# An RK4 loop with an FFN in its slots: the unclipped q goes through PSUM, the seed goes ahead of the clip, and five FFN sums move from GpSimd to VectorE

## The reference, cut to what matters

```
def _derivative(q, p, drive, coupling, bias):
    dq = q - q ** 3 / 3.0 - p + drive + jnp.tanh(q) @ coupling.T + bias
    dp = EPSILON * (q + ALPHA - BETA * p)
...
q_next = q + DT / 6.0 * (dq1 + 2 * dq2 + 2 * dq3 + dq4)
q_next = jnp.clip(q_next, -CLAMP, CLAMP)          # CLAMP = 20, the same for p_next
...
qx, sx, sc = _reorder_quantize_x(xf, up_reorder_index)      # fp8 rounding, one scale a row
g = _qlinear(qx, sx, sc, w_gate, ...); u = _qlinear(qx, sx, sc, w_up, ...)
t = jax.nn.silu(g) * u
qt, st, sct = _reorder_quantize_x(t, down_reorder_index)
y = _qlinear(qt, st, sct, w_down, down_reorder_index)
```

## Time and profile before

| | |
|---|---|
| median of 3 runs | 1775.01 us (1772.31 to 1779.2) |
| the profiled execution, its own time | 1778.82 us, span 1777.0 us |
| TensorE busy | 1558.6 us, 88% |
| VectorE busy | 1146.7 us, 65% |
| ScalarE busy | 486.2 us, 27% |
| GpSimd busy | 383.7 us, 22% |
| DMA | 70.26 MB, mean 40 GB/s |

### The profile page before, as it was taken

How to read it: one execution, slowest core, us unless ns; L and a number is a source line. 1 busy time by engine, 2 the same in 40 slices (tenths; PEclk the granted TensorE clock), 3 DMA queues, 4 the chain that set the end, 5 groups by cost and what they waited for, 6 DMA issues and landing times.

```text
span 1777.0 us, 44630 instructions
## 1 busy us (share of the span) xinstructions
PE 1558.6 (88%) x16703; PEld 960.7 (54%) x16744; DVE 1146.7 (65%) x3063; ACT 486.2 (27%) x1333; POOL 383.7 (22%) x554
## 2 busy tenths in 40 slices
PE   5999899998869999999999996778788888888884
PEld 2333333333747667676676744555565555555552
DVE  2888633335687556475664713478888888888885
ACT  1323211112020210202102012344444444444442
POOL 1221000000000000000000001245455445545554
PEclk9999999999879999999999998899999999999997
DMA  7232200005000000000000032011111111111111
GB/s 302 72 83 72 62 24 12 12 10 107 1 0 1 24 6 18 24 0 24 6 18 24 0 118 94 20 29 32 34 34 30 32 30 32 30 30 36 38 29 36
DMA packets 88431, 70.26 MB, mean 40 GB/s; under 512 B 30728, under 2 KB 80824, under 8 KB 87352
## 3 DMA queue, kind: packets, MB, share of 16 engines
q1 hardware_dynamic: 86616, 63.75, 12.5%
q0 software_dynamic: 1760, 5.77, 1.2%
HBM read 52.55 MB, written 16.92 MB: 39 GB/s over the span
## 4 chain that ended last, share of the span: by engine, by line
PE 66%; DVE 17%; issue 7%; ACT 5%; DMA 2%; SPq 1%; POOL 1%; DVEq 1%; ACTq 0%; POOLq 0%
PE ps L681 12%; PE ps L671 12%; PE ps L774 12%; PE ps L588 9%; PE ps L596 8%; DVE mem L1311 4%; PE ps L715 3%; PE ps L739 2%; DVE mem L1318 2%; ACT ps L955 2%; DVE ps L1289 2%; ACT mem L962 2%; DMA mem<-in_xT 1%; DVE mem L1322 1%; PE ps L692 1%
## 5 line engine op out<-in xcount | busy, mean ns | idle before, releaser
L774 PE MATMUL ps<-mem 128*32 128x128 f32 x8192 | 284.5, 280 | 122.2 <-ACT mem L962 55.1
L774 PEld LDWEIGHTS ps<-mem 128*32 128x32 f32 x8192 | 220.2, 111 | 196.1 <-issue 119.5
L671 PE MATMUL ps<-mem 128*128 128x512 f32 x512 | 224.6, 592 | 0.0
L681 PE MATMUL ps<-mem 128*128 128x256 f32 x1024 | 222.3, 379 | 0.0
L681 PEld LDWEIGHTS ps<-mem 128*128 128x128 f32 x1024 | 193.9, 190 | 26.0
L514 POOL TENSOR_TENSOR mem<-mem 128x128 f32<-128x128 f32 x64 | 31.2, 487 | 802.5 <-ACT mem L958 802.5
L588 PE MATMUL ps<-mem 128*32 128x384 f32 x2048 | 184.2, 502 | 0.0
L596 PE MATMUL ps<-mem 128*32 128x384 f32 x2048 | 177.1, 486 | 2.7 <-DVE mem L1120 2.7
L671 PEld LDWEIGHTS ps<-mem 128*128 128x128 f32 x512 | 95.6, 190 | 109.7 <-issue 109.3
L518 POOL TENSOR_TENSOR mem<-mem 128x128 f32<-128x128 f32 x192 | 103.7, 540 | 191.5 <-ACT mem L958 185.4
L765 PE MATMUL ps<-mem 128*128 128x128 f32 x768 | 141.0, 308 | 0.0
(11 more groups left out here) (128 smaller groups left out, 2103.5 us busy)
## 6 DMA issues: line engine op xcount, KB each, us to landing
mem<-x_scr SPq DMA_DIRECT2D x128, 64.0 KB, 1.9
mem<-in_xT SPq DMA_DIRECT2D x64, 64.0 KB
mem<-in_Wq SPq DMA_DIRECT2D x1, 4096.0 KB
mem<-in_Wo SPq DMA_DIRECT2D x1, 4096.0 KB
mem<-in_x SPq DMA_DIRECT2D x16, 256.0 KB, 2.7
x_scr<-mem SPq DMA_DIRECT2D x32, 128.0 KB, 2.3
q_scr<-mem SPq DMA_DIRECT2D x64, 64.0 KB, 1.6
mem<-q_scr SPq DMA_DIRECT2D x64, 64.0 KB, 1.9
```

The source lines that it names most:

```text
L671: mm = pe.matmul(ps[:, 6 + pr, :], aoT[:, h, pr * P:pr * P + P], wo[:, h, :], start=(h == 0), stop=(h == HEADS - 1))
L681: mm = pe.matmul(ps[:, h % Q_BANKS, 0:BLK], wq[:, c, h * DH:(h + 1) * DH], xnb[:, c, :], start=(c == 0), stop=(c == NC - 1))
L774: mm = pe.matmul(ps[32 * j:32 * j + 32, st % 2, 0:P], thT[:, c, :], ct[:, c, j * P:(j + 1) * P], start=False, stop=(c == NC - 1), skip_gro ...
```

## The change

In the fourth stage the new q is written to an unused part of PSUM bank 4 instead of the SBUF tile `qpre`. The transpose and the clip read it there. The seed of the next step's first stage is issued ahead of the clip, no longer at the start of the next stage. Five sums of a tile leave POOL for VectorE: the two of 512 columns of the q rounding (now slots 8 and 9), the two `t_rounded` halves of 768 and 640 columns (slots 13 and, one group on, 0) and the last sum with x1 (slot 14 instead of 11). POOL keeps the sums of p and `gate_scaled`.

```diff
--- before.py
+++ after.py
@@ -247,7 +247,7 @@
         qst = [f32(w.take(P), P) for _ in range(3)]
         qsT = f32(w.take(P), NC, B)
         thT = f32(w.take(P), NC, B)
-        ebuf, qpre, pacc = (f32(w.take(P), P) for _ in range(3))
+        ebuf, pacc = (f32(w.take(P), P) for _ in range(2))
         pw = [f32(w.take(P), P) for _ in range(5)]
         qt = f32(w.take(D), D)
         x1t = f32(w.take(D), D)
@@ -528,39 +528,15 @@
                 pool.wait_ge(f_sig, GU_T * i + m + 1)
                 pool.tensor_tensor(sig[m % 2], sig[m % 2], us_row[:, m * GU_N:(m + 1) * GU_N], ALU.mult).then_inc(f_sgu, 1)
 
-            def t_rounded(i, half):
-
-                lo, hi = T_PARTS[half]
-                pool.wait_ge(f_ta, 2 * i + half + 1)
-                wait_if(pool, f_tT, 2 * i + half - 1)
-                pool.tensor_tensor(t8[:, lo:hi], vt[:, lo:hi], et[:, lo:hi], ALU.subtract).then_inc(f_t8, 1)
-
             def slot(k, tile):
                 i = tile(0)
                 if i is not None:
-                    if k == 7:
-                        pool.wait_ge(f_xe, i + 1)
-                        pool.tensor_tensor(vq, vq, eq, ALU.add).then_inc(f_xa, 1)
-                    if k == 8:
-                        pool.wait_ge(f_xa, i + 1)
-
-                        wait_if(pool, f_qT, i)
-                        pool.tensor_tensor(qx8, vq, eq, ALU.subtract).then_inc(f_q8, 1)
                     if k in (13, 14):
                         gate_scaled(i, k - 13)
                 i = tile(1)
                 if i is not None:
                     if k in (1, 3):
                         gate_scaled(i, 2 + k // 2)
-                    if k in (12, 15):
-                        t_rounded(i, k // 15)
-                i = tile(2)
-                if i is not None and k == 11:
-                    pool.wait_ge(f_ysc, i + 1)
-                    pool.wait_ge(x1_ld, 16 * TILE_T * (i + 1))
-
-                    wait_if(pool, o_wr, PRIMED + 16 * TILE_T * i)
-                    pool.tensor_tensor(yout, ysc, x1t, ALU.add).then_inc(f_out, 1)
 
             def group(g, rk, tile):
                 for k in range(16):
@@ -1289,6 +1265,7 @@
                     dve.scalar_tensor_tensor(out=o, in0=p, scalar=float(SEEDS[st][0]), in1=driven(s), op0=ALU.mult, op1=ALU.add).then_inc(rk_seed, 1)
 
             drive_sum(0, 0, 1)
+            seed(0, 0, 0)
 
             def stage(g, s, st, last, fill):
                 t = 4 * g + s
@@ -1296,8 +1273,6 @@
                 qs = qn[(s - 1) % 4] if st == 0 else qst[st - 1]
                 stt = dve.scalar_tensor_tensor
                 end = last and s == 3
-                if st == 0:
-                    seed(t, s, 0)
                 dve.wait_ge(rk_sq, n + 1)
                 stt(out=ebuf, in0=ps[:, 5, 0:P], scalar=KEPT[st], in1=qs, op0=ALU.subtract, op1=ALU.mult).then_inc(rk_e, 1)
                 if st < 3:
@@ -1307,7 +1282,7 @@
                     drive_sum(t + 1, (s + 1) % 4, g + 1 + (s == 3))
                 dve.wait_ge(rk_e, n + 1)
                 dve.wait_ge(rk_mm, n + 1)
-                dst = qst[st] if st < 3 else qpre
+                dst = qst[st] if st < 3 else ps[:, 4, 2 * P:3 * P]
                 stt(out=dst, in0=ps[:, st % 2, 0:P], scalar=STEP[st], in1=ebuf, op0=ALU.mult,
                     op1=ALU.subtract).then_inc(rk_qs if st < 3 else rk_pre, 1)
                 if st < 3:
@@ -1317,9 +1292,11 @@
                 if not (end and st == 3):
                     dve.transpose(qsT.rearrange("p c b -> p (c b)"), dst).then_inc(rk_qT, 1)
                 if st == 3:
+                    if not end:
+                        seed(t + 1, (s + 1) % 4, 0)
 
                     wait_if(dve, q_wr[s], PRIMED + 16 * g)
-                    dve.tensor_scalar(qn[s], qpre, CLAMP, -CLAMP, ALU.min, ALU.max).then_inc(rk_qs, 1)
+                    dve.tensor_scalar(qn[s], dst, CLAMP, -CLAMP, ALU.min, ALU.max).then_inc(rk_qs, 1)
 
             def slot(v, k, tile):
 
@@ -1341,6 +1318,14 @@
                         dve.wait_ge(f_vq, PRIMED + i + 1)
                         v.need(v.did(dve.tensor_scalar(eq.bitcast(U32), vq.bitcast(U32), EXP_BITS, None, ALU.bitwise_and)))
                         dve.tensor_scalar(eq, eq, FP8_TINY, ROUND_AT, ALU.max, ALU.mult).then_inc(f_xe, 1)
+                    if k == 8:
+                        dve.wait_ge(f_xe, i + 1)
+                        dve.tensor_tensor(vq, vq, eq, ALU.add).then_inc(f_xa, 1)
+                    if k == 9:
+                        dve.wait_ge(f_xa, i + 1)
+
+                        wait_if(dve, f_qT, i)
+                        dve.tensor_tensor(qx8, vq, eq, ALU.subtract).then_inc(f_q8, 1)
                     if k in (12, 13):
                         gate_part(i, k - 12)
                     if k == 14:
@@ -1370,9 +1355,19 @@
                         t_grid(v, 1)
                     if k == 11:
                         t_added(v, 0)
+                    if k == 13:
+                        t_rounded(i, 0)
                     if k == 15:
                         t_added(v, 1)
                 i = tile(2)
+                if i is not None and k == 0:
+                    t_rounded(i, 1)
+                if i is not None and k == 14:
+                    dve.wait_ge(f_ysc, i + 1)
+                    dve.wait_ge(x1_ld, 16 * TILE_T * (i + 1))
+
+                    wait_if(dve, o_wr, PRIMED + 16 * TILE_T * i)
+                    dve.tensor_tensor(yout, ysc, x1t, ALU.add).then_inc(f_out, 1)
                 if i is not None and k == 10:
                     v.need(v.n)
                     dve.wait_ge(f_y, i + 1)
@@ -1397,6 +1392,13 @@
                 lo, hi = T_PARTS[half]
                 v.need(v.n)
                 dve.tensor_tensor(vt[:, lo:hi], vt[:, lo:hi], et[:, lo:hi], ALU.add).then_inc(f_ta, 1)
+
+            def t_rounded(i, half):
+
+                lo, hi = T_PARTS[half]
+                dve.wait_ge(f_ta, 2 * i + half + 1)
+                wait_if(dve, f_tT, 2 * i + half - 1)
+                dve.tensor_tensor(t8[:, lo:hi], vt[:, lo:hi], et[:, lo:hi], ALU.subtract).then_inc(f_t8, 1)
 
             def gate_part(i, m):
```

## The result

The changed kernel takes 1784.8 us (median of 7 runs, 1783.9 to 1788.0) against 1775.3 before: a ratio of 1.0057, 95% interval 1.0044 to 1.0070. It is 9.5 us slower. The profiled execution has a span of 1782.6 us.

A forecast was written before the change was run, and what follows sets the result against it. The RK4 loop was taken as latency bound, 2.33 us a stage, with most loss from POOL collisions. Sums +44.3, removed -29.9 and tail -4 gave +10.4 us: 1785.4 against the median 1775.0, range 1771 to 1793.

The forecast's parts named there:

- That POOL's sum and VectorE's SBUF instruction exclude one another, the first starter winning: RK4 loop: one engine holds something exclusively for an instruction's length; the clip took 1.09 instead of 0.18 us under POOL's sum.
- What goes, 29.9 us: RK4 loop: collided clips and the delayed mask behind POOL's long sums, 33.0 - 1.35 - 4.6 + 2.8 us removed.
- That the earlier seed by itself is worth nothing: First stage of a step without collision: TensorE waits for tanh, which the seed already beats, so no gain.
- The clip's price: Clip reading PSUM takes 0.29 us instead of 0.18; slot work at +1.81 instead of +1.59, still covered.
- The estimate of 65 ns more: Transpose reading PSUM: 65 ns more each, 4 us for 63; the forecast costed nothing, following the trace instead.
- The five sums: Sums moved to VectorE lengthen intervals into slots 0, 8, 9, 13, 14: 44.3 us together, bound 24.7 without contention.
- the race of slot 14: POOL's second product starts 0.13 us ahead of the output sum and holds it: over by 1.03, 13.4 us.
- my fallback for VectorE winning the race (2.69): Rival: output sum goes first, interval into slot 14 is 2.69 us; 9.1 less, 1776.3 us; chance 0.30.
- SP's queue at nothing: Output sum three slots later makes SP wait longer ahead of tile stores, x1 loads and a q store: costs nothing.
- the tail: Behind the last stage, POOL's sums are in the chain itself; moving them gives -4 us (-2 to -5.5).
- the gain of 1.2 that was forecast for the clip: Tail: the last clip no longer waits 1.35 us, of which some 1.2 reach the q store.
- The signs of being wrong: Moved sums not stretched, ScalarE's square no longer following the clip, or TensorE's granted clock falling in the longer stages.

The follow-up runs named there:

- seed_psum_only: Kernel before with only new q through PSUM and seed ahead of clip; the five sums stay on POOL: 1757.2 us, ratio 0.9907.
- seed_first_sbuf: Kernel before with only the seed ahead of the clip; unclipped q in SBUF, sums on POOL: 1782.6 us, one run.
- yout_first: Changed kernel with the output sum ahead of gated_part in slot 14: 1782.8 us, ratio 1.0045 to the kernel before.
- yout_pool: Changed kernel with the output sum back on POOL in slot 11: 1777.1 us, ratio 1.0013 to the kernel before.
- sums_only: Kernel before with only the five sums moved to VectorE; clip and seed as before: 1781.2 us, ratio 1.0038.
- p_held: Changed kernel with POOL's two second-stage sums of p held until the third stage's copy is there: 1775.3 us, one run.
- p_later: Changed kernel with POOL's two second-stage sums of p issued in the third stage, their waits already fulfilled in the second: 1787.7 us, one run.
- both: Kernel before with q through PSUM, seed ahead of clip, slot 8's mask ahead of the seed and ScalarE's qxT copy in slot 11: 1734.0 us, ratio 0.9768.
- drive_first: Changed kernel with the output sum back on POOL and the drive's sum ahead of the slot's work: 1770.4 us, one run.
- bits_early: Kernel before with q through PSUM, seed ahead of clip, and slot 8's mask ahead of the next seed: 1749.6 us, ratio 0.9849.
- copy_later: Kernel before with q through PSUM, seed ahead of clip, and ScalarE's qxT copy moved from slot 10 to 11: 1743.8 us, ratio 0.9827.
- after_sbuf: Changed kernel with the unclipped q in SBUF again, seed still ahead of the clip: 1782.7 us, one run.

## Why the prediction was right

The forecast was +10.4 us, 1785.4; measured +9.5, 1784.8. Point by point:

- **That POOL's sum and VectorE's SBUF instruction exclude one another, the first starter winning.** Shown, by the clip's 0.27 under L543 once it reads PSUM, by the mask's 1.64 and 0.55 at 0.05 behind and 0.15 ahead, and by slot 9 with and without POOL's sums. Who is first is less sharp than the records: 0.04 behind won in the earlier trace rows, 0.05 behind lost in seed_psum_only.
- **What goes, 29.9 us.** In the changed kernel the clip is constant, and what slots 8 and 0 are still over is the moved sums'. Over all groups of before the intervals into slots 0, 4 and 8 were 13.1, 2.9 and 13.9 us over 2.33, 29.9 together; of a steady group it is 2.25.
- **That the earlier seed by itself is worth nothing.** True of the undisturbed stage it was read from, but not of the held ones: in seed_first_sbuf the order alone took 0.22 off slots 0 and 4 each, and put 0.79 on slot 12.
- **The clip's price.** 0.29 taken, 0.275 measured; slot work at 1.79 instead of 1.81. The transpose with PSUM as its source took 0.316 against 0.312 on the mean, within the bound of 0.02. The estimate of 65 ns more that the prediction made from the Trainium skill, "VectorE: DVE Perf Modes", section "The TRN2 errata", does not show in these transpositions.
- **The five sums.** Excess over 2.33 in slots 0, 8, 9, 13 and 14: 0.67, 0.51, 0.71, 0.26 and 1.02 where 0.71, 0.56, 0.74, 0.25 and 1.03 stood. With the counts of the prediction (13, 14, 14, 14, 13) that makes 42.7 against 44.3. POOL won the race of slot 14, by 0.16. The intervals that the prediction lists add up to a group of 41.6, not the 41.7 it states; measured 41.59.
- **Slot 14's reason was only half told.** The number came out, but the drive's sum, which I had costed at its free length, has two SBUF inputs too. Undoing the output sum gave back 0.60, not 1.02; and my fallback for VectorE winning the race (2.69) would have been too low (in yout_first, where the output sum does go first, the drive's sum is held and the slot takes 3.11).
- **SP's queue at nothing.** Wrong in the tail. The output tile is ready three slots later, so its stores and the x1 loads (L442, 1737.06 to 1738.94) stand ahead of the last q store L427, which leaves 1.50 behind the last new q, 0.87 after the clip has ended. Before, held up by the clip, it left at 1.89; in yout_pool, where the output sum is back in slot 11, it leaves at 0.65, which is the gain of 1.2 that was forecast for the clip. The reload L435 is issued sooner than before as well (2.03 behind the new q instead of 2.36), but its last part lands 3.25 after its issue instead of 1.86. So VectorE waits 2.40 us and its reduction starts 6.67 behind the last new q, against 5.60 before and 4.37 in yout_pool. Of the 2.3 us between this and yout_pool 0.85 are the queue; why the last part lands so late no run shows. From the scaling of the down product to the end of the span the tail took 15.1 instead of 18.0 (L1376 at 1767.48, L1381 at 1759.00), 2.9 less where 2.7 was forecast; the tail as a whole gave 2.5 instead of 4.
- **The slot 6 interval**, 2.44 instead of 2.33 in the groups of the hardware loop and not in those written out (2.33 in groups 0, 1, 2 and 15), was not foreseen: 0.11 in 11 groups and 0.35 in the first of them, 1.6 us. It appears in the steady groups of each kernel with both the sums on VectorE and the seed ahead, and in none of the others. Its cause is open: VectorE's instructions there start and end as in sums_only, and only the new q behind them starts 0.11 later.
- **The signs of being wrong.** The output sum was stretched, the square follows the clip, and from group 2 on the granted clock of every stage of the changed kernel is 1.00.

From the first new q to the last the profiled execution took 647.7 us before and 657.3 after, +9.5. The terms give 42.7 for the sums, -29.9 for what went, 1.6 for slot 6, -4.3 for five fewer stages at TensorE's lower clock (last section) and -0.5 for the interval behind the last of these in the kernel before (3.87 against 3.34), 9.6 together. With the tail's -2.5 and 1.5 less ahead of the loop, where nothing was changed, that is the 5.6 by which the spans differ. The medians differ by 9.5, since the profiled execution of before was itself 3.5 above its median and that of the changed kernel 0.4 below.

That the total is within 1 us of the forecast is in part luck. Without the stages at the lower clock, which the prediction did not have, the terms as measured make 42.7 - 29.9 + 1.6 - 2.5 = +11.9, and the medians differ by 9.5; the 2.4 between is less than what those stages differ by among the profiled executions, though no profile shows it of the timed ones. The sums were put 1.6 too high, the tail 1.5 too good, and slot 6 was left out: two of the three errors ran against the third.

## What to carry to other kernels

Before moving work from GpSimd to VectorE to end their collisions, see if the held instruction can take its input from PSUM: here that freed a 128-column clip for 0.1 us, while moving the sums put 3.2 us a group more into VectorE's slots than they could hide. When one stall is removed, list everything behind it in the same queue by its operands, down to the shortest; a 128-column sum of two SBUF tensors inherited 0.4 us of a wait. And in a latency-bound ring, an order on a side engine (the copy ahead of the square) can be worth nearly as much as the contention: 13 us here, beside the 17 of the freed clip.

## What the runs showed of the hardware that I had not expected

The start of the RK4 loop runs partly at TensorE's lower clock, and how much differs among the profiled executions. The first group of the kernel before and then of the changed one (stretch, us; busy us and count of PE, PEld, DVE, ACT, POOL; granted clock; DMA share, GB/s):

```profile
1081.70:1122.40 40.70, 30.70 (x561) 24.17 (x562) 18.83 (x72) 13.12 (x52) 8.48 (x20) 0.82 0.16 58
```

```profile
1080.20:1118.50 38.30, 26.69 (x562) 21.06 (x562) 19.13 (x73) 13.56 (x52) 8.48 (x20) 0.95 0.17 61
```

```profile
1082.90:1084.60 1.70, 1.70 (x32) 1.41 (x32) 0.00 (x0) 0.18 (x1) 0.90 (x2) 0.50 0.91 364
```

The last line is the inside of one such stage of before: a granted clock of 0.50, which is the lower of the two levels, 1.2 instead of 2.4 GHz. Eight stages of before, at first one in each step, show 1.93 us for their 32 matmuls instead of 1.08, and an interval of 3.19 instead of 2.33; the changed kernel has three. I see no tie to the change: counting each stage whose matmuls take 1.85 us or more, p_held has eight, seed_first_sbuf, sums_only, p_later, both and drive_first seven, bits_early six, copy_later five, seed_psum_only, yout_pool and yout_first four, after_sbuf three, whatever their order of seed and clip. At 0.86 us a stage this is a difference of up to 4 us. The timed runs of one kernel spread as far (1772.3 to 1779.2, 1783.9 to 1788.0), and with the mean granted clock: of 30 other timings of the kernel before, the three with a clock of 0.977 took 1770.1 to 1771.7 us and the three with 0.970 took 1777.4 to 1779.9. It is why intervals of a steady group were compared above and not only totals.
